# Three of 28 columns of the first multi-head pass picked by TensorE through two PSUM banks

## What is computed

```
for i in range(3):
    q, k, v = (h @ Wq[i]), (h @ Wk[i]), (h @ Wv[i])          # 4 heads of 16
    scores = sum over a head of q[dst] * k[src] / 4 + e @ We[i]
    p = exp(scores - segment_max(scores, dst)[dst])
    agg = segment_sum(p / denom[dst] * v[src], dst)
    h = layernorm(h + agg @ Wo[i])
    e = layernorm(e + gelu(concat(h[src], h[dst], e) @ Wem[i] + bem[i]))
```

## Time and profile before

| | us |
|---|---|
| median of 3 runs | 10206.79 (10204.67 to 10208.48) |
| profiled execution, its time | 10210.79 |
| its span in the trace | 10209.0 |
| TensorE's mean granted clock | 0.789 of full speed |
| POOL, DVE, PE, ACT busy | 73%, 72%, 65%, 55% |

### The profile page before, as it was taken

How to read it: one execution, slowest core, us unless ns; L and a number is a source line. 1 busy time by engine, 2 the same in 40 slices (tenths; PEclk the granted TensorE clock), 3 DMA queues, 4 the chain that set the end, 5 groups by cost and what they waited for, 6 DMA issues and landing times. The chain is left out here.

```text
span 10209.0 us, 106412 instructions
## 1 busy us (share of the span) xinstructions
PE 6617.0 (65%) x29219; PEld 5572.4 (55%) x29219; DVE 7363.6 (72%) x13024; ACT 5584.2 (55%) x6064; POOL 7477.5 (73%) x7352
## 2 busy tenths in 40 slices
PE   6888878859978996996997688621114333343333
PEld 5776767748867885885886577621113222232222
DVE  8777666657766775776777799845554788858887
ACT  2555556657766775775776456523332455535553
POOL 7888867767767776776776777677776777677774
PEclk8899879979988997997998688855555666656665
DMA  6544433322322332332454355434443555545553
GB/s 226 92 81 81 77 94 79 81 63 74 87 79 59 89 85 52 87 89 64 117 142 131 102 136 139 117 107 131 131 139 100 181 184 188 168 131 183 184 188 101
DMA packets 792292, 1183.93 MB, mean 116 GB/s; under 512 B 472967, under 2 KB 547571, under 8 KB 784515
## 3 DMA queue, kind: packets, MB, share of 16 engines
q0 software_dynamic: 322752, 363.08, 17.9%
q1 hardware_dynamic: 405373, 470.66, 15.1%
q10 hardware_dynamic: 64070, 349.10, 8.5%
HBM read 733.35 MB, written 461.77 MB: 117 GB/s over the span
## 5 line engine op out<-in xcount | busy, mean ns | idle before, releaser
L1165 POOL DMA_INDIRECT turned<-d_t,idx x5788 | 5483.2, 947 | 1823.8 <-issue 1753.3
L1310 PE MATMUL banks<-pair,hot 128*128 128x462 f32 x16184 | 3479.9, 376 | 185.1 <-DVE wide L1431 139.0
L1310 PEld LDWEIGHTS banks<-pair,hot 128*128 128x128 f32 x16184 | 3059.3, 190 | 604.7 <-DVE wide L1431 204.5
L1366 PE MATMUL banks<-ident,wide 128*128 128x128 f32 x588 | 160.5, 417 | 1585.0 <-ACT wide L1185 867.4
L928 ACT ACTIVATE hot<-keys,row 128x1024 fp32r<-128x1024 f32 (+1 forms) x1036 | 1073.4, 1117 | 150.4 <-PE banks L1310 72.8
L847 POOL DMA_INDIRECT d_acc<-work,idx x560 | 956.2, 1707 | 194.1 <-issue 165.3
L1641 DVE TENSOR_TENSOR_SCAN wide<-banks,wide 128x224 f32<-128x224 f32 (+4 forms) x1288 | 1037.5, 872 | 5.8
L1366 PEld LDWEIGHTS banks<-ident,wide 128*128 128x128 f32 x588 | 101.0, 209 | 1660.7 <-ACT wide L1185 897.9
L1279 ACT COPY wide<-wide 128x952 f32<-128x952 f32 (+2 forms) x252 | 502.4, 1994 | 844.1 <-DVE wide L1641 844.1
L939 ACT ACTIVATE hot<-hot 128x3584 fp32r<-128x3584 f32 (+1 forms) x296 | 907.7, 3115 | 0.6
L1431 DVE TENSOR_TENSOR wide<-banks,member 128x462 f32<-128x462 f32 x1156 | 670.4, 633 | 284.2 <-PE banks L1310 251.0
(11 more groups left out here) (352 smaller groups left out, 9790.7 us busy)
## 6 DMA issues: line engine op xcount, KB each, us to landing
d_e<-wide ACTq DMA_DIRECT2D x168, 924.0 KB
turned<-d_t,idx POOLq DMA_INDIRECT x5788
d_e<-wide ACTq DMA_DIRECT2D x84, 1008.0 KB
wide<-d_b SPq DMA_DIRECT2D x60, 1344.0 KB
keys<-d_key SPq DMA_DIRECT2D x124, 512.0 KB, 4.0
keys<-d_edge_key SPq DMA_DIRECT2D x203, 256.0 KB, 4.5
d_b<-wide SPq DMA_DIRECT2D x28, 1344.0 KB, 8.7
wide<-d_edge SPq DMA_DIRECT2D x84, 448.0 KB, 6.3
```

Of the source, the lines that this page charges most:

```text
L1165: gp.indirect_dma_start(rows[:, b, k, :], None, table[:, :], offset(idx[:, b, k:k + 1])).then_inc(s["gathered"][b], 16)
L1310: mm = nc.tensor.matmul(ps_cols[i], hot[:, place, i, j, :], flat(g.pair[:, part, j]), start=(j, part) == (0, 0), stop=(j, part) == (SETS - ...
```

## The change

The first multi-head pass gets 3 of its 28 columns from TensorE and gathers 25. What goes with it:

- ACT makes the one-hots one edge column at a time (`column_hot`) in a ring of two places: for chunk c+3 (counted from 1, as the code does; it is two chunks on from the loop's number) the first two right behind the store of chunk c's state, the third in the next turn behind the save of the edge product.
- PE picks a column in two half rows of 64 words, into banks 3 and 7, each half waiting until DVE has taken the same half of the column before (`ring_columns`). It does so behind the edge product of the chunk.
- DVE takes each half by a product and a sum (`ring_take`): column 0 behind the exponents' arguments, column 1 behind the product of values and weights, column 2 behind the scans. `found` lies in the buffer `prod`.
- To free banks 3 and 7: `keep` is spread to 4 mask rows for each head instead of 8, so DVE does 16 scans of 112 words instead of 8 of 224; and the edge product and the logits go to banks 1 and 2 by separate matmuls of 128 and 16 words instead of one of 144.
- `b_rows`, keys and mask lie in the node state buffer `g.h`. The copy of the node state into it, made by DVE for each node group before (L1924), is made once by POOL at the end of the pass.
- In the node part DVE splits the table in two parts (`split_set`), and the keys are loaded behind the last normalisation.

```diff
@@ Picks
+        if self.ring:
+            self.keys = g.h[:, K:K + 2 * X, :].rearrange("p (x a) e -> p x a e", a=2)
+            self.member = g.h[:, K + 2 * X:K + 3 * X, 0:SET]
+            self.hot = ph.sbuf("hot", [P, HOT_RING, SETS, P], F32R)
+            self.pair = ph.sbuf("pair", [P, 2, SETS, KF, SET], F32R)
...
+def column_hot(nc, g, act, pk, n, i, slot, first=False):
+    q = pk.X * (n - 1) + i
+    if not first:
+        act.wait_ge(pk.s["cols_done"], 2 * (q - 1))
+    act.wait_ge(pk.s["keys_loaded"], 16 * n)
+    for j in range(SETS):
+        last = nc.scalar.activation(pk.hot[:, slot, j, :]..., pk.keys[:, i], ACT.Abs, ...)
+    last.then_inc(pk.s["hot_link"], 1)
+    act.wait_ge(pk.s["hot_link"], q + 1)
+    nc.scalar.activation(part, part, ACT.Relu, ...).then_inc(pk.s["hot_made"], 1)
...
@@ edges
-        FR = HF // 2
+        FR = HF // 4 if ring else HF // 2
...
+            ps_half = [banks[:, i, 0:SET * HALF] for i in (3, 7)]
+    ps_logits = banks[:, 2, 3 * P:3 * P + 16 * G4]
...
@@ gpsimd, at the end
+        if ring:
+            gp.wait_ge(s["b_turned"], CHUNKS + 2)
+            gp.wait_ge(picks["cols_taken"], 2 * X * CHUNKS)
+            nc.gpsimd.tensor_copy(g.h, g.x).then_inc(s["h_kept"], 1)
...
@@ tensor
+        def ring_columns(n, b, first=False):
+            for i in range(X):
+                q = X * (n - 1) + i
+                pe.wait_ge(picks["hot_made"], q + 1)
+                for h in range(2):
+                    if not first or i:
+                        pe.wait_ge(picks["cols_taken"], 2 * (q - 1) + h + 1)
+                    for j in range(SETS):
+                        for part in range(2):
+                            mm = nc.tensor.matmul(ps_half[h], hot[...], flat(pk.pair[:, part, j, h half, :]), ...)
+                    mm.then_inc(picks["cols_done"], 1)
...
@@ build
-        layer(nc, g, dict(kind="dot", rows=g.x, copy=g.h, weights=a["l3_w0"], ...
-                          seed=(g.d_q64, D)), dict(kind="multi", a=w_edges(0)))
+        layer(nc, g, dict(kind="dot", rows=g.x, lent=True, weights=a["l3_w0"], ...
+                          seed=(g.d_q64, D)), dict(kind="multi", a=w_edges(0), ahead=0, cols=MULTI_COLS))
```

More of the change, by code:

```diff
@@ L862 @@
 KF_RING = 3
+HOT_RING = 2
 AHEAD = 2
@@ L1215, in _ @@
         act.dma_start(prime[0:1, 0:1], g.d_x[0:1, 0:1]).then_inc(s["stored"], 16)
-        for n in range(2, AH + 3 if X and not dot else 2):
+        for n in range(2, AH + 3 if X and kind == "gat" else 2):
             one_hots(nc, g, act, pk, n, n % 2, n == 2)
@@ L1254, in one @@
                 copy_logits(chunk)
-            if X and not dot and more:
+            if kind == "gat" and more:
                 one_hots(nc, g, act, pk, chunk + AH + 3, (b + AH + 1) % 2)
@@ L1266, in one @@
                 save_product(chunk, cols)
-            if X and not dot and more:
+            if ring and (more or b == 0):
+                for i in range(HOT_RING, X):
+                    column_hot(nc, g, act, pk, chunk + 2, i, (X * (b + 1) + i) % HOT_RING)
+            if kind == "gat" and more:
                 one_hots_end(nc, act, pk, chunk + AH + 3, (b + AH + 1) % 2)
@@ L1285, in one @@
                 half_hots(nc, g, act, pk, chunk + 3, 0)
+            if ring and more:
+                for i in range(HOT_RING):
+                    column_hot(nc, g, act, pk, chunk + 3, i, (X * (b + 2) + i) % HOT_RING)
         pairs(act, one)
@@ L1444, in _ @@
                 wide_take(1, 0, i, link)
-        if not X or dot:
+        if ring:
+            link = Link(v, s["first_link"])
+            for i in range(X):
+                ring_take(1, 0, i, link)
+        if not X or dot or ring:
             v.wait_ge(ready["spread_done"], 16 * C)
@@ L1515, in spread_em @@
             last.then_inc(s["em_spread"], 1)
-        if X and not dot:
+        if kind == "gat":
             link = Link(v, s["first_link"])
@@ L1615, in one @@
             nc.vector.tensor_copy(maxima[:, :, 0:1], maxima[:, :, K:K + 1])
-            if X and not dot and (more or b == 0):
+            if ring and (more or b == 0):
+                ring_take(chunk + 2, 1 - b, 0, link)
+            if kind == "gat" and (more or b == 0):
                 take(chunk + AH + 2, 1 - b, KG, 0, EARLY, link)
@@ L1626, in one @@
                 wide_take(chunk + 2, 1 - b, 1, link)
+            if ring and (more or b == 0):
+                ring_take(chunk + 2, 1 - b, 1, link)
             if update:
@@ L1649, in one @@
                 wide_take(chunk + 2, 1 - b, 3, link)
-            elif X and (more or b == 0):
+            elif ring and (more or b == 0):
+                for i in range(2, X):
+                    ring_take(chunk + 2, 1 - b, i, link)
+            elif kind == "gat" and (more or b == 0):
                 take(chunk + AH + 2, 1 - b, KG, EARLY, X, link)
```

125 lines of the change are left out of this document (105 added, 20 removed).

## The result

| | us |
|---|---|
| changed kernel, median of 4 runs | 10270.12 (10261.24 to 10271.34) |
| kernel before, median of 4 runs | 10205.73 (10200.33 to 10208.48) |
| ratio, 95% interval | 1.0062 (1.0047 to 1.0077) |
| profiled execution after: time, span | 10269.41, 10267.7 |

What follows compares the result with a forecast made beforehand. POOL's own pace (35.04 us a chunk) was taken as the bound before, a 38.3 us chain through DVE, ACT and PE after. +83 for 26 steps, -7, -1 and +1 gave +76: 10283 us, range 10190 to 10325.

Steps and rivals of the forecast that it cites:

- 3 two one-hots, table load: ACT, ahead of turn_e: two new one-hots take 6.2 us, a table load 0.64 on average, reaching 21.5 us.
- 5 product ends; L1729 starts: PE's edge product takes 6.0 us, to 28.8; after drain and ACT's logits copy DVE may start at 29.3.
- 8 next L1751: DVE takes half 1 and copies the weights; the next product of values and weights starts at 37.7 or 38.9 us.
- The chain: From one chunk's product of values and weights to the next, through DVE, ACT and PE: 38.3 us, 3.2 more; chance 71%.
- step 7: PE starts column 0 at half clock, rising after 3.3 or 5.9 us: half 0 at 33.4 or 34.2, half 1 36.2 or 37.4.
- The last step: Last of the 27 steps between chunks, with no one-hots ahead and no columns: about -7 us.
- POOL's copy of the node state: At the pass's end: 2.8 us, at most twice that, covered by DVE's last chunk: 0, or +6 if the cover failed.
- The node part: DVE's table split in 7 steps hidden by POOL's queue: 0, some 4 us if its last group came late.
- the first chunk: Starts 3.75 us earlier and takes one column before its product of values and weights: -1 us.
- The product did not lift the clock: Rival: PE's narrow passes bring the full clock, a chunk takes 34.5 to 35.8 us, total 10187 to 10219; chance 20%.
- the clock did not fall: Rival: PE's clock falls between columns, about 45 us a chunk if at half all through, total 10470; chance 6%.
- POOL's pace: Rival: POOL keeps the pace, everything fits under 31.28 us a chunk, total 10105; chance 3%.

Runs made afterwards that it cites:

- e2: Changed kernel with only the second of the two one-hots moved from between chunks to behind the next chunk's logits copy: 10166.52 us, 0.9984 of the kernel before.
- e7: Changed kernel with both one-hots moved directly behind the next turn_e, ahead of the mask copy: 10097.3 us, ratio 0.9911 to before; on slower chips 1.0120 to 1.0132.
- e4: Changed kernel with two columns on PE instead of three, POOL gathering 26: 10255.15 us, ratio 1.0068 to the kernel before.
- e1: Changed kernel with both one-hots moved into the next chunk, the first behind the mask copy, the second behind the logits copy: 10209.17 us, ratio 1.0023 to before.
- e3: Changed kernel plus 48 extra PE matmuls while PE waits for turn_e, output unchanged: 10186.06 us, ratio 1.0004 to the kernel before.
- e5: Changed kernel with the product's seven 16-word products replaced by one of 112 words: 13703.66 us on a slower chip, ratio 1.0118 to the kernel before.

## Why the prediction was right

Times from the start of L1751, in the chunk shown, which has a table load; the forecast is the prediction's with the load's 0.64 made a full 1.28.

| step | forecast | trace |
|---|---|---|
| 1 state done | 11.7 | 11.6 |
| 2 state copied, next instruction | 14.6 | 14.6 |
| 3 two one-hots, table load | 22.1 | 22.1 |
| 4 product starts | 23.4 | 23.4 |
| 5 product ends; L1729 starts | 29.4; 29.9 | 29.2; 29.8 |
| 6 ready for column 0 | 32.7 | 32.3 |
| 7 half 0, half 1 taken | 34.0 to 34.8, 36.8 to 38.0 | 33.7, 36.5 |
| 8 next L1751 | 38.3 to 39.5 | 38.0 |

- **The chain** stands as written, through ACT's one-hots, `turn_e`, the product, the logits' copy and column 0. e2, e7 and e4 show it by what they take away: 3 us a chunk, 6 us a chunk, and a column that costs nothing.
- **The mis-sized term is step 7.** I took the middle of 3.3 and 5.9 us for the clock's rise. Half 0 was there 4.43 us after PE began column 0 (7253.30 - 7248.87), 4.82 in the chunk before it; 14 matmuls at the full clock with the signal are about 3.0, so some 8 to 10 of them were at 0.373, for 3.0 to 3.9 us. The granted clock says the same: it rose some 2.8 us after 7248.87 (0.64 in 7251 to 7252 us, 1.00 behind it), and some 3.7 us after the 7210.47 of the chunk before (0.91 in 7214 to 7215 us). The lower end held. The chunks without a table load take 37.05, not 1.28 less than 38.0 but 0.97. Two chunks together take 37.5 each, against 38.3: 26 steps gave 66.8 us instead of 83.
- **The last step** is 7809.86 - 7782.64 = 27.22 against 35.14 before, -7.9 where -7 stood.
- **POOL's copy of the node state** takes 2.80 us and ends under the scans, as forecast; L1751 to the join of the pass is 17.06 us against 16.82.
- **The node part was costed at 0 and takes 7.5 us.** This term failed. From the pass's join to the transfer of the seed it is 132.9 us before (6621.33 to 6754.27) and 140.4 now (6616.11 to 6756.50). POOL's transfers in it, before and after:

```profile
L2073 POOL DMA_INDIRECT wide<-d_e,idx_last x49 | 48.0, 980 | 16.2 <-issue 14.6 <-DMA d_e<-merged,idx_join 1.5
L2080 POOL DMA_INDIRECT d_b<-wide,idx_first x49 | 47.1, 962 | 14.9 <-issue 14.6 <-ACT wide L2017 0.3
```
```profile
L2222 POOL DMA_INDIRECT d_b<-wide,idx_first x49 | 51.7, 1055 | 14.9 <-issue 14.9
L2215 POOL DMA_INDIRECT wide<-d_e,idx_last x49 | 51.0, 1041 | 16.1 <-issue 14.6 <-DMA d_e<-merged,idx_join 1.5
```

49 x (0.093 + 0.061) = 7.5. Of that, 6.8 us are in seven transfers of 1.73 to 2.44 us instead of 0.95, one beside each of the seven subtractions of the split (L992); before, no transfer of this node part took over 1.33. I had asked whether DVE's new work could make POOL wait for its results; it could not. It made POOL's own instructions longer, and POOL sets the pace there. The trace of before had it, in the node part of the dot pass, where the table was split already: L2080 at 1121 ns. I compared the waits there, not the durations.
- **The sum:** 66.8 - 7.9 + 7.5 - 0.9 (the first chunk) + 0.2 = 65.7, of which 7.0 went back outside these terms: 58.7. 4.0 of them lie ahead of the dot pass; where they come from isn't shown. Two errors, 16 us too much and 7.5 too little, partly hid each other.
- **The rivals.** The product did not lift the clock by its end; whether its passes helped the rise to come at the early end is not shown. Columns 1 and 2 ran at the full clock (84 matmuls in 18.72 us), so the clock did not fall. Only in e7 did a step come down to POOL's pace (31.5 against 31.28), with DVE level beside it; what had stood in the way was 6 us of ACT's order and no work.

## What to carry to other kernels

Work that an engine has slack for still costs its full length if it is put ahead of what another engine is about to ask for; look for the instruction on which the others wait, and put new work behind it, but not behind a wait of its own (e1). When an engine's own pace is the bound, compare the durations of its instructions in stretches with and without the neighbour's work, not only its waits. And a saving off the chain comes back as a wait at the chain's next meeting point: e4 is the cheap way to see that.

## What the runs showed of the hardware

In the node part of the kernel after, DVE's subtraction with two inputs in SBUF holds up a POOL transfer that starts beside it until 0.7 us after its end (L992 ends at 6704.85 + 1.78 = 6706.63, the transfer at 6707.34), while the cast ahead of it, equally long, does not:

```profile
6703.24 1.76 DVE L991 CAST pair<-wide 128x896 fp32r<-128x896 f32 x1
6703.63 0.96 POOL L2222 DMA_INDIRECT d_b<-wide,idx_first  x1 [0.30 <-issue]
6704.85 1.78 DVE L992 TENSOR_TENSOR pair<-wide 128x896 fp32r<-128x896 f32 x1
6704.90 2.44 POOL L2222 DMA_INDIRECT d_b<-wide,idx_first  x1 [0.30 <-issue]
```

The Trainium skill ("SBUF — State Buffer", "Who interferes with whom") says that a DVE instruction with two SBUF inputs contends with a GpSimd instruction that reads SBUF. By that rule, the trace agrees.

In e3 TensorE's clock stayed at 2.4 GHz over 1.48 us of idle time (granted 1.00 throughout). In the other sort of chunk, behind 2.80 us of idle time, it fell to 1.2 GHz within the first microsecond of the product (0.69, then 0.50).

At either level a pass of 16 words takes as long as one of 128. In the kernel after, the weight loads of the product start 0.43 us apart for two passes of either width (7243.26, 7243.68, 7244.11 us), so 0.21 each, and e5's twelve narrow passes cost 0.216 each. In e3 at the full clock it is 0.22 to 0.23 for two (7247.77, 7247.99, 7248.22 us), so 0.11 each.
